# Attention scores as three row-tiled products per head, two heads at a time, in a fused attention and mixture-of-experts kernel

## The chip, the cores and the metric

The kernel runs on one core of a Trainium2 chip. The metric is the device time of one execution in microseconds, as a median over runs. TensorE (PE in the profile) multiplies; its weight loads are shown apart as PEld. VectorE is DVE, ScalarE is ACT, GpSimd is POOL, SyncE is SP.

## The reference

A normalised x attends to a context of 512 rows per batch: 16 query heads in 4 groups, head size 64. Then comes a layer of 32 experts, of which each token takes 8.

```python
def xattn(q, k, v, Wc, bc):                       # 16 batches, 512 queries, 512 keys
    qh = q.reshape(b, s, 4, 4, 64).transpose(0, 2, 3, 1, 4)
    kh = k.reshape(b, s, 4, 64).transpose(0, 2, 1, 3)
    vh = v.reshape(b, s, 4, 64).transpose(0, 2, 1, 3)
    scores = jnp.einsum('bghsd,bgtd->bghst', qh, kh) / sqrt(64)
    probs = jax.nn.softmax(scores, axis=-1)
    out = jnp.einsum('bghst,bgtd->bghsd', probs, vh)
    return out.transpose(0, 3, 1, 2, 4).reshape(b, s, 1024) @ Wc.T + bc
x = x + xattn(layernorm(x), ctx, ctx, Wc, bc)
x = x + moe(layernorm(x))                         # top 8 of 32 experts, 1024 -> 384 -> 1024
```

## The kernel before

It has four stages: a setup, attention, a schedule of expert tiles, and the experts. The change touches attention alone.

Attention works through 64 tiles of 128 queries, 4 to a batch. The first and the last batch are written out, the 14 between are turns of a loop whose body holds 4 tiles. Every engine has its own program, and each walks the 16 heads of a tile as steps h = 0 to 15. Semaphores alone tie the engines together.

Scores need more precision than one product of type fp32r gives, so queries and keys are split into a high and a low part. Of each head, qT holds the high part on array rows 0 to 63 and the low part on rows 64 to 127. The keys stand twice: kT has high over low, kT_swapped low over high. Two products over all 128 rows (lines 798 and 799) then give all four partial products of one head.

What TensorE does in step h, in this order:

- scores of head h + AHEAD, with AHEAD = 3: two products of 512 columns into bank h % 2 of two (S_BANK). It waits until the exponent of head h + 1, which read that bank last, is done.
- transpose_probs (line 813): four transposes of the probabilities of head h.
- in odd steps, values (line 836): half of the product of probabilities and values of the group before. Its output has 64 partitions, and two of these products stand side by side in the 64-column halves of the array.
- as tables of steps say, project (line 855): three products of 512 columns for each 128 rows of the output projection of the tile before, here one such chunk in most steps, two in steps 7 and 8, none in 5 and 6; then transposes of the second normalised rows (line 871, steps 4 and 5), the router (line 877, step 6), and transposes of the next tile's queries (line 776, steps 10 to 13).

What ScalarE does in step h: copy_probs (line 487, except in steps 1, 5, 9, 13, where VectorE does it on line 607), the exponent of head h + 3 (line 479), then extras: the high part of the output (496) in steps 1, 5, 9, 13, the second norm (502) in step 3, copies of its transposes (509) in 4 and 5, the next first norm (448) in 6, the high part of the next queries (455) in 7, and copies of their transposes (460) in 10 to 13.

What VectorE does in step h: the maximum of head h + 3 (line 592), then extras: 607 and the low part of the output (621, after ScalarE's 496) in steps 1, 5, 9, 13; statistics (570, 574) in 1, 2, 11 and 15; the choice of experts (642 to 652) in 7, (658) in 11, (665) in 13; places and entries of the table in 3 and 5; the residual (632) in 8 and 15. GpSimd does the low part of the next queries (393), the bias (399), small norm factors and scatters.

Of the kernel before, what the change touches and what calls it, by code (L numbers as in the profile page):

```python
# [56 lines left out]
def moe_block(nc, x, ctx_in, Wc, bc, gate_w, gate_proj, up_proj, down_proj, out):  # L57
# [36 lines left out]
    with top:  # L94
# [13 lines left out]
        with attention_mem:  # L108
# [17 lines left out]
            xq = sb(attention_mem, "xq", [P, H, 2, HEAD_DIM], F32R)  # L126
# [3 lines left out]
            kT = sb(attention_mem, "kT", [P, G, 512], F32R)  # L130
            kT_swapped = sb(attention_mem, "kT_swapped", [P, G, 512], F32R)
# [54 lines left out]
            scores_done, max_ready, exp_ready = sem("scores_done"), sem("max_ready"), sem("exp_ready")  # L186
# [167 lines left out]
            def _(pool):  # L354
# [35 lines left out]
                def queries_lo(i):  # L390

                    hold(xq_hi_ready, i + 1)
                    pool.tensor_tensor(xq[:, :, 1, :], xn[:, :].rearrange("p (h d) -> p h d", d=HEAD_DIM),
                                       xq[:, :, 0, :].bitcast(F32), ALU.subtract).then_inc(xq_ready, 1)
# [49 lines left out]
            def _(act):  # L444
# [6 lines left out]
                def queries_hi(i):  # L451

                    act.wait_ge(xn_ready, i + 1)
                    wait(act, qt_done, 4 * i)
                    act.activation(xq[:, :, 0, :], xn[:, :].rearrange("p (h d) -> p h d", d=HEAD_DIM), ACT.Copy
                                   ).then_inc(xq_hi_ready, 1)
# [110 lines left out]
            def _(dve):  # L567
# [14 lines left out]
                def keys_lo(b, g, half):  # L582

                    dve.wait_ge(khi_copied, 2 * (G * b + g) + half + 1)
                    rows = slice(half * HEAD_DIM, (half + 1) * HEAD_DIM)
                    lo, hi = (kT_swapped, kT) if half == 0 else (kT, kT_swapped)
                    dve.tensor_tensor(lo[rows, g, :], O_BANK[g % 2][rows, :], hi[rows, g, :].bitcast(F32), ALU.subtract
                                      ).then_inc(klo_copied, 1)

                def maximum(i, h):  # L590
                    dve.wait_ge(scores_done, H * i + h + 1)
# [106 lines left out]
                def tile(t):  # L698
                    i = t.i
                    for h in range(H):  # L700
# [4 lines left out]
                        for b, g in groups_at(t, h - 1, KEYS):  # L705
                            keys_lo(b, g, 1)
# [10 lines left out]
                        for b, g in groups_at(t, h, KEYS):  # L717
                            keys_lo(b, g, 0)
# [25 lines left out]
                for g in range(2):  # L744
                    for half in range(2):
                        keys_lo(0, g, half)
# [17 lines left out]
            def _(pe):  # L764
                def transpose_queries(i, n):
# [23 lines left out]
                def scores(b, s, i, h):  # L789
# [4 lines left out]
                    if h % 4 == 0 and s == 0:  # L794
                        pe.wait_ge(khi_copied, 2 * (G * b + g + 1))
                        pe.wait_ge(klo_copied, 2 * (G * b + g + 1))
# [875 lines left out]
```

## Time and profile before

| what | us |
|---|---|
| median of 3 runs | 9384.93 |
| lowest and highest | 9379.66, 9392.39 |
| the profiled execution | 9424.62 |
| its span | 9422.8 |
| PE busy, share of the span | 97% |
| DVE, ACT, POOL busy | 68%, 45%, 56% |

The profile is of one execution, 0.4% over the median. An engine counts as busy from an instruction's start to its end, and matmuls overlap each other's ends, so PE's throughput is read from the starts of its instructions and not from their durations.

### The profile page before, as it was taken

Reading aid. Unit: us, or ns where it says so; the run is one execution under the profiler, and the core shown is the slowest. Engines: PE = TensorE matmul, PEld = TensorE weight load, DVE = VectorE, ACT = ScalarE, POOL = GpSimd, SP = SyncE. Lnnn points to the kernel's source line nnn. Section 1 sums busy time; section 2 is a strip of 40 time slices with the busy share of each in tenths; the row PEclk is TensorE's granted clock in tenths of the full one; section 3 lists DMA queues with packets and bytes.
Section 4 is the critical chain, followed back from the end, with each engine's and each line's share of the span. In section 5 each row is a group of like instructions: output and inputs, shape, how many; then the busy total and the mean of one; then the engine's idle time right before and its main releaser. Section 6 shows DMA issues by size and latency. Waiting matters only on the chain.

```text
span 9422.8 us, 173720 instructions
## 1 busy us (share of the span) xinstructions
PE 9114.1 (97%) x46640; PEld 7509.9 (80%) x46641; DVE 6400.5 (68%) x9216; ACT 4227.1 (45%) x7011; POOL 5243.0 (56%) x4825
## 2 busy tenths in 40 slices
PE   8999999999969999999999999999999999999999
PEld 5777777777747888888888888888888888888888
DVE  5666666666646767777666667677777667766676
ACT  6666666666633433333333333333333333333333
POOL 2444444444445656666556566565666566656564
PEclk9999999999979999999999999999999999999999
DMA  2222212112114545555454455455555455544554
GB/s 96 59 57 59 61 55 63 58 55 64 57 60 105 117 106 115 116 124 128 109 111 110 111 132 114 108 113 114 117 116 127 105 121 114 116 107 111 127 113 82
DMA packets 787085, 926.16 MB, mean 98 GB/s; under 512 B 403473, under 2 KB 600081, under 8 KB 786578
## 3 DMA queue, kind: packets, MB, share of 16 engines
q0 software_dynamic: 209920, 604.72, 29.8%
q1 hardware_dynamic: 430866, 165.82, 7.1%
q10 hardware_dynamic: 145920, 151.01, 5.0%
q8 instruction: 184, 3.01, 0.1%
q14 instruction: 195, 1.60, 0.1%
HBM read 1076.32 MB, written 376.45 MB: 154 GB/s over the span
## 4 chain that ended last, share of the span: by engine, by line
PE 63%; DVE 3%; issue 2%; ACTq 1%; another core or an unknown queue 0%; ACT 0%; POOL 0%; DMA 0%; DVEq 0%; SPq 0%; POOLq 0%
PE bank L1581 41%; PE bank L1604 22%; DVE gu_lo L1495 1%; DVE xT L1484 1%; DVE xT_lo L1489 0%; ACTq L1383 0%; DVE h L1507 0%; DVE h_hi L1510 0%; DVE h_lo L1512 0%; ACTq L1375 0%; POOL xg L1329 0%; ACT xT_hi L1396 0%; DVE d_lo L1500 0%; DVE rows_out L1519 0%
## 5 line engine op out<-in xcount | busy, mean ns | idle before, releaser
L1329 POOL DMA_INDIRECT xg<-xn_rows,gather_row x2304 | 2970.1, 1289 | 1882.5 <-PE bank L1581 1271.4
L1581 PE MATMUL bank<-xT_hi,gu_hi 128*128 128x512 f32 (+2 forms) x6912 | 2557.1, 370 | 118.2 <-DVE xT_lo L1489 107.7
L1581 PE MATMUL bank<-xT_lo,gu_hi 128*128 128x512 f32 (+2 forms) x6912 | 2544.6, 368 | 0.0
L1581 PE MATMUL bank<-xT_hi,gu_lo 128*128 128x512 f32 (+2 forms) x6912 | 2544.5, 368 | 0.0
L1414 ACT ACTIVATE gated<-bank 128x512 f32<-128x512 f32 x432 | 258.6, 599 | 3047.0 <-PE bank L1581 2826.9
L1581 PEld LDWEIGHTS bank<-xT_hi,gu_hi 128*128 128x128 f32 x6912 | 1300.4, 188 | 302.1 <-issue 95.7
L1341 POOL DMA_INDIRECT out_rows<-rows_out,entry_now x576 | 1101.7, 1913 | 682.3 <-DVE rows_out L1519 399.0
L1581 PEld LDWEIGHTS bank<-xT_lo,gu_hi 128*128 128x128 f32 x6912 | 1300.7, 188 | 158.2
L1581 PEld LDWEIGHTS bank<-xT_hi,gu_lo 128*128 128x128 f32 x6912 | 1300.1, 188 | 158.8
L1604 PE MATMUL bank<-d_hi,h_hi 128*128 128x512 f32 x3162 | 1247.1, 394 | 53.7 <-DVE h_lo L1512 41.8
L1484 DVE STREAM_TRANSPOSE xT<-xg 128x512 f32<-128x512 f32 x1152 | 1284.1, 1156 | 13.6 <-DMA xg<-xn_rows,gather_row 13.6
L1604 PE MATMUL bank<-d_hi,h_lo 128*128 128x512 f32 x3162 | 1235.8, 391 | 0.0
L1604 PE MATMUL bank<-d_lo,h_hi 128*128 128x512 f32 x3162 | 1235.4, 391 | 0.0
L592 DVE TENSOR_REDUCE neg_max<-bank 128x1 f32<-128x512 f32 x1024 | 703.7, 687 | 568.0 <-PE bank L799 464.2
L1495 DVE TENSOR_TENSOR gu_lo<-gu_raw,gu_hi 128x2048 fp32r<-128x2048 f32 x432 | 973.5, 2284 | 151.0 <-ACT gu_hi L1403 90.6
L1507 DVE TENSOR_TENSOR h<-bank,gated 128x512 f32<-128x512 f32 x432 | 296.9, 687 | 1105.7 <-ACT gated L1414 913.2
L411 POOL DMA_INDIRECT slot_table<-entry,slot_i x512 | 507.8, 992 | 706.1 <-ACT pT L487 530.8
L479 ACT ACTIVATE probs<-bank,neg_max 128x512 f32<-128x512 f32 x1024 | 701.9, 685 | 344.8 <-DVE neg_max L592 300.5
L1403 ACT ACTIVATE gu_hi<-gu_raw 128x2048 fp32r<-128x2048 f32 x432 | 809.3, 1908 | 58.3 <-DMA gu_raw<-in_L_ffn_up_proj 58.3
L1519 DVE TENSOR_SCALAR rows_out<-bank,entry_now 128x512 f32<-128x512 f32 x576 | 430.8, 748 | 583.6 <-PE bank L1604 580.8
L1396 ACT ACTIVATE xT_hi<-xT 128x512 fp32r<-128x512 f32 x1152 | 673.5, 622 | 300.9 <-issue 276.3
L1489 DVE TENSOR_TENSOR xT_lo<-xT,xT_hi 128x512 fp32r<-128x512 f32 x1152 | 750.9, 684 | 77.2 <-ACT xT_hi L1396 77.2
(160 smaller groups left out, 12733.6 us busy)
## 6 DMA issues: line engine op xcount, KB each, us to landing
d_raw<-in_L_ffn_down_proj ACTq DMA_DIRECT2D x144, 1536.0 KB
gu_raw<-in_L_ffn_gate_proj ACTq DMA_DIRECT2D x145, 1024.0 KB
gu_raw<-in_L_ffn_up_proj ACTq DMA_DIRECT2D x145, 1024.0 KB
gu_raw<-in_L_ffn_gate_proj ACTq DMA_DIRECT2D x145, 512.0 KB
gu_raw<-in_L_ffn_up_proj ACTq DMA_DIRECT2D x145, 512.0 KB
xg<-xn_rows,gather_row POOLq DMA_INDIRECT x2304
x_t<-in_x SPq DMA_DIRECT2D x64, 512.0 KB, 4.8
inv_wide<-inverse_sums SPq DMA_DIRECT2D x512, 64.0 KB
```

The lines of the kernel that those rows point to most:

```text
L411: pool.indirect_dma_start(out=table, out_offset=bass.IndirectOffsetOnAxis(ap=slot_i[:, k:k + 1], axis=0), in_=entry[:, k, :], in_offset=No ...
L479: act.activation(probs[h % 4][:, :], S_BANK[h % 2][:, :], ACT.Exp, bias=neg_max[:, h:h + 1], accum_out=row_sum[:, h:h + 1]).then_inc(exp_r ...
L592: dve.tensor_reduce(neg_max[:, h:h + 1], S_BANK[h % 2][:, :], AX.X, ALU.max, negate=True).then_inc(max_ready, 1)
L1329: pool.indirect_dma_start(out=xg[:, m, :], out_offset=None, in_=quarter_rows, in_offset=bass.IndirectOffsetOnAxis(ap=gather_row[:, m:m + 1 ...
L1341: pool.indirect_dma_start(out=out, out_offset=bass.IndirectOffsetOnAxis(ap=entry_now[:, q, 0:1], axis=0), in_=rows_out[:, q, :], in_offset ...
L1396: act.activation(xT_hi[:, c, :], xT[:, c, :], ACT.Copy).then_inc(xt_hi, 1)
L1403: act.activation(gu_hi[:, :, :, cols], gu_raw[:, :, :, cols].rearrange("p n c m -> p c n m"), ACT.Copy).then_inc(guhi_ready, 1)
L1484: dve.transpose(xT[:, :, 2 * pair * QUAD:2 * (pair + 1) * QUAD].rearrange("p c (m r) -> p m c r", r=QUAD), xg[:, 2 * pair:2 * pair + 2, :] ...
L1489: dve.tensor_tensor(xT_lo[:, c, :], xT[:, c, :], xT_hi[:, c, :].bitcast(F32), ALU.subtract).then_inc(xt_lo, 1)
L1495: dve.tensor_tensor(gu_lo[:, :, :, cols], gu_raw[:, :, :, cols].rearrange("p n c m -> p c n m"), gu_hi[:, :, :, cols].bitcast(F32), ALU.su ...
L1581: last = nc.tensor.matmul(bank[:, 0:cols], w[:, c, n, j * P:(j + 1) * P], v[:, c, 0:cols], start=(c == 0 and w is gu_hi and v is xT_hi), s ...
L1604: last = nc.tensor.matmul(D_BANK[q][n][:, 0:cols], v[:, k, q * P:(q + 1) * P], w[:, k, n * 512:n * 512 + cols], start=(k == ks[0] == 0 and ...
```

## The change

Queries: xq keeps the whole high row and then the whole low row, no longer side by side for each head. One transpose of 128 columns then holds two heads, the even one on rows 0 to 63 and the odd one on rows 64 to 127; qT[:, h] of an even h is the high part of both and qT[:, h + 1] their low part. Keys: the high part stands on both halves of kT_hi, the low part on both halves of kT_lo; ScalarE writes the one in one instruction (two before), VectorE the other in one (two before).

Scores come two heads at a time, in odd steps: high by high, high by low and low by high of each head, each over 64 array rows, the even head into bank 0 and the odd head into bank 1. The low by low product is gone. The call waits for the exponents of both heads that used the banks before.

The step order of TensorE changes: scores and the query transposes of an odd step come first in it; two chunks of the projection stand in every even step, at its end, behind the transposes of the second norm and the router.

```diff
-            PROJECT = {0: (1, 0, 1, 2), 1: (1, 0, 2, 3), 2: (1, 0, 3, 4), 3: (1, 0, 4, 5), 4: (1, 0, 5, 6), 7: (1, 0, 6, 8),
-                       8: (1, 1, 0, 2), 9: (1, 1, 2, 3), 10: (1, 1, 3, 4), 11: (1, 1, 4, 5), 12: (1, 1, 5, 6), 13: (1, 1, 6, 7),
-                       14: (1, 1, 7, 8), 15: (0, 0, 0, 1)}
+            PROJECT = {h: (1, h // GROUP_HEADS // 2, h % 8, h % 8 + 2) for h in range(0, H, 2)}
...
-                    act.activation(kT[0:HEAD_DIM, g, :], O_BANK[g % 2][0:HEAD_DIM, :], ACT.Copy).then_inc(khi_copied, 1)
-                    act.activation(kT_swapped[HEAD_DIM:P, g, :], O_BANK[g % 2][HEAD_DIM:P, :], ACT.Copy).then_inc(khi_copied, 1)
+                    act.activation(kT_hi[:, g, :], O_BANK[g % 2][:, :], ACT.Copy).then_inc(khi_copied, 1)
...
+                    dve.tensor_tensor(kT_lo[:, g, :], O_BANK[g % 2][:, :], kT_hi[:, g, :].bitcast(F32), ALU.subtract
...
-                                                   xq[:, 4 * n + k, :, :].rearrange("p two d -> p (two d)"), ident_r[:, :])
+                                                   xq[:, k % 2, (2 * n + k // 2) * P:(2 * n + k // 2 + 1) * P], ident_r[:, :])
...
-                    wait(pe, exp_ready, H * i + h - 1)
-                    nc.tensor.matmul(S_BANK[h % 2][:, :], qT[s % 2][:, h, :], kT[:, g, :], start=True, stop=False)
-                    nc.tensor.matmul(S_BANK[h % 2][:, :], qT[s % 2][:, h, :], kT_swapped[:, g, :], start=False, stop=True
-                                     ).then_inc(scores_done, 1)
+                    wait(pe, exp_ready, H * i + h)
+                    for part, keys in ((0, kT_hi), (0, kT_lo), (1, kT_hi)):
+                        for r in range(2):
+                            rows = slice(HEAD_DIM * r, HEAD_DIM * (r + 1))
+                            last = nc.tensor.matmul(S_BANK[r][:, :], qT[s % 2][rows, h + part, :], keys[rows, g, :],
+                                                    start=(part == 0 and keys is kT_hi), stop=(part == 1))
+                            if part == 1:
+                                last.then_inc(scores_done[r], 1)
...
                     for h in range(H):
-                        if h + AHEAD < H:
-                            scores(t.b, t.s, i, h + AHEAD)
-                        elif t.next:
-                            scores(t.next_b, t.next_s, i + 1, h + AHEAD - H)
+                        if h % 2:
+                            scores_ahead(t, h)
+                            queries_at(t, h)
                         transpose_probs(i, h)
...
-                        if h in PROJECT and (t.back1 or not PROJECT[h][0]):
-                            back, n, c0, c1 = PROJECT[h]
-                            project(i - back, n, list(range(c0, c1)))
                         if h in TRANSPOSE2 and t.back2:
                             transpose_xn2(i - 2, TRANSPOSE2.index(h))
                         if h == ROUTER and t.back2:
                             router(i - 2)
-                        if h in NEXT_QUERIES and t.next:
-                            transpose_queries(i + 1, NEXT_QUERIES.index(h))
+                        if h % 2 == 0:
+                            project_at(t, h)
+                            queries_at(t, h)
```

On TensorE, steps 3 and 4 of a tile, without their first and last rows, stood like this before (798 and 799 are scores, 813 transposes of probabilities, 836 values, 855 the projection, 871 transposes of the second norm):

```order
L813 MATMUL bank<-ident,probs 128x128 x4
L836 MATMUL bank<-pT,v 64x256 x4
L855 MATMUL bank<-WcT_hi,oT_hi 128x512
L855 MATMUL bank<-WcT_lo,oT_hi 128x512
L855 MATMUL bank<-WcT_hi,oT_lo 128x512
L41 REGISTER_ALU
L798 MATMUL bank<-kT,qT 128x512
L799 MATMUL bank<-kT_swapped,qT 128x512
L41 REGISTER_ALU
L813 MATMUL bank<-ident,probs 128x128 x4
L855 MATMUL bank<-WcT_hi,oT_hi 128x512
```

The same place now, steps 3 and 4 (791 is scores, 807 the transposes of probabilities, 830 values, 865 those of the second norm, 849 the projection):

```order
L791 MATMUL bank<-kT_hi,qT 128x512 x2
L791 MATMUL bank<-kT_lo,qT 128x512 x2
L791 MATMUL bank<-kT_hi,qT 128x512 x2
L807 MATMUL bank<-ident,probs 128x128 x4
L830 MATMUL bank<-pT,v 64x256 x4
L807 MATMUL bank<-ident,probs 128x128 x4
L865 MATMUL bank<-ident,xn 128x128 x4
L849 MATMUL bank<-WcT_hi,oT_hi 128x512
L849 MATMUL bank<-WcT_lo,oT_hi 128x512
```

Scores, transposes, values and transposes now follow each other, and the projection stands in one piece behind them, just ahead of the next scores.

ScalarE's order does not change in these steps; of the changed kernel, steps 7 and 8 (474 exponent, 452 high part of the next queries, 482 copy of transposed probabilities):

```order
L474 ACTIVATE probs,row_sum<-bank,neg_max 128x512
L41 REGISTER_ALU
L452 ACTIVATE xq<-xn 128x1024
L482 ACTIVATE pT<-bank 128x4x128
L470 REGISTER_ALU
L474 ACTIVATE probs,row_sum<-bank,neg_max 128x512
```

The exponent at the end of this piece is the one for which TensorE's scores of step 9 now wait; before, it was the one at its head.

## Rows read from the trace of the kernel before

**Rows 1.** Stretches: start:end, length, busy PE, PEld, DVE, ACT, POOL, clock, DMA share, GB/s.

```profile
144.00:2723.00 2579.00, 2502.41 (x15730) 1851.87 (x15729) 1695.88 (x3837) 1709.29 (x3816) 1117.95 (x1846) 0.99 0.20 58
1350.00:1397.70 47.70, 42.66 (x261) 31.05 (x261) 30.70 (x68) 30.74 (x69) 18.13 (x30) 0.96 0.15 49
1397.70:1437.10 39.40, 39.40 (x252) 29.24 (x251) 27.06 (x61) 27.19 (x61) 18.20 (x30) 1.00 0.17 52
```

**Rows 2.** Timeline (start us, length us, instruction, [idle before]), PE: the router, once a tile.

```profile
1437.14 1.91 PE L877 MATMUL bank<-gate_sb,xn2T 128*128 128x32 f32 x16
1476.65 1.91 PE L877 MATMUL bank<-gate_sb,xn2T 128*128 128x32 f32 x16
```

**Rows 3.** Timeline, PE: steps 8 and 9 of an ordinary tile.

```profile
1442.97 0.60 PE L813 MATMUL bank<-ident,probs 128*128 128x128 f32 x4
1443.32 0.48 PE L855 MATMUL bank<-WcT_hi,oT_hi 128*128 128x512 f32 x1
...
1445.03 0.39 PE L799 MATMUL bank<-kT_swapped,qT 128*128 128x512 f32 x1
1445.26 0.60 PE L813 MATMUL bank<-ident,probs 128*128 128x128 f32 x4
1445.79 1.08 PE L836 MATMUL bank<-pT,v 128*64 128x256 f32 x8
1446.81 0.50 PE L855 MATMUL bank<-WcT_hi,oT_hi 128*128 128x512 f32 x1
1447.14 0.40 PE L855 MATMUL bank<-WcT_lo,oT_hi 128*128 128x512 f32 x1
```

**Rows 4.** Groups by line in attention: weight loads of 64 and of 128 columns.

```profile
L836 PEld LDWEIGHTS bank<-pT,v 128*64 128x64 f32 x3960 | 241.0, 136 | 156.2 <-issue 84.9
L799 PEld LDWEIGHTS bank<-kT_swapped,qT 128*128 128x128 f32 x982 | 187.0, 190 | 24.6
```

**Rows 5.** Timeline, ACT, of the same tile.

```profile
1441.30 1.06 ACT L455 ACTIVATE xq<-xn 128x1024 fp32r<-128x1024 f32 x1
1443.60 0.60 ACT L487 ACTIVATE pT<-bank 128x512 f32<-128x512 f32 x1 [1.24 <-PE bank L813]
1444.10 0.68 ACT L479 ACTIVATE probs<-bank,neg_max 128x512 f32<-128x512 f32 x1
1444.66 0.20 ACT L479 ACTIVATION_READ_ACCUMULATOR probs<-bank,neg_max 128x1 f32 x1
...
1446.19 0.69 ACT L479 ACTIVATE probs<-bank,neg_max 128x512 f32<-128x512 f32 x1 [1.04 <-DVE neg_max L592]
...
1446.87 0.41 ACT L496 ACTIVATE oT_hi<-o_norm 128x256 fp32r<-128x256 f32 x1
...
1471.36 1.23 ACT L502 ACTIVATE xn<-x,ln 128x1024 f32<-128x1024 f32 x1
```

**Rows 6.** Timeline, DVE, of the same tile.

```profile
1445.46 0.69 DVE L592 TENSOR_REDUCE neg_max<-bank 128x1 f32<-128x512 f32 x1 [0.68 <-issue]
1446.07 0.68 DVE L607 COPY pT<-bank 128x512 f32<-128x512 f32 x1
1447.30 1.50 DVE L621 TENSOR_TENSOR oT_lo<-o_norm,oT_hi 128x256 fp32r<-128x256 f32 x1 [0.56 <-ACT oT_hi L496]
...
1457.36 0.42 DVE L621 TENSOR_TENSOR oT_lo<-o_norm,oT_hi 128x256 fp32r<-128x256 f32 x1 [0.69 <-issue]
1457.70 0.60 DVE L665 TENSOR_REDUCE chosen<-hot 128x32 bf16<-128x256 f32 x1
...
1460.78 0.68 DVE L632 TENSOR_TENSOR x<-bank,x_t 128x512 f32<-128x512 f32 x1
1462.34 0.21 DVE L574 BATCH_NORM_AGGREGATE mv<-bn 128x2 f32<-128x12 f32 x1 [0.16 <-DVE bn L570]
```

**Rows 7.** Timeline, POOL, of the same tile.

```profile
1446.11 2.40 POOL L399 TENSOR_TENSOR x_t<-x_t,bias_row 128x1024 f32<-128x1024 f32 x1
```

**Rows 8.** Timeline, DVE, where the loop turns.

```profile
1548.85 0.69 DVE L592 TENSOR_REDUCE neg_max<-bank 128x1 f32<-128x512 f32 x1 [4.72 <-issue]
```

More of the change, by code:

```diff
@@ L125, in moe_block @@
             xn = sb(attention_mem, "xn", [P, D], F32)
-            xq = sb(attention_mem, "xq", [P, H, 2, HEAD_DIM], F32R)
+            xq = sb(attention_mem, "xq", [P, 2, D], F32R)
             qT = [sb(attention_mem, f"qT{n}", [P, H, P], F32R) for n in range(2)]
@@ L129, in moe_block @@
             v = sb(attention_mem, "v", [P, TC, G, HEAD_DIM], F32)
-            kT = sb(attention_mem, "kT", [P, G, 512], F32R)
-            kT_swapped = sb(attention_mem, "kT_swapped", [P, G, 512], F32R)
+            kT_hi = sb(attention_mem, "kT_hi", [P, G, 512], F32R)
+            kT_lo = sb(attention_mem, "kT_lo", [P, G, 512], F32R)
             probs = [sb(attention_mem, f"probs{n}", [P, 512], F32) for n in range(4)]
@@ L184, in moe_block @@
             khi_copied, klo_copied = sem("khi_copied"), sem("klo_copied")
-            scores_done, max_ready, exp_ready = sem("scores_done"), sem("max_ready"), sem("exp_ready")
+            scores_done, max_ready, exp_ready = [sem(f"scores_done{n}") for n in range(2)], sem("max_ready"), sem("exp_ready")
             inverse_turned = sem("inverse_turned")
@@ L454, in queries_hi @@
                     wait(act, qt_done, 4 * i)
-                    act.activation(xq[:, :, 0, :], xn[:, :].rearrange("p (h d) -> p h d", d=HEAD_DIM), ACT.Copy
-                                   ).then_inc(xq_hi_ready, 1)
+                    act.activation(xq[:, 0, :], xn[:, :], ACT.Copy).then_inc(xq_hi_ready, 1)
                 def copy_queries(i, s, n):
@@ L580, in statistics1, with keys_lo @@
                     statistics(n, ln1_chain, 2 * i, bn1, mv1, x_t[s], stats1)
[L582 to L587, printed above, removed]
+                def keys_lo(b, g):
+                    dve.wait_ge(khi_copied, G * b + g + 1)
+                    dve.tensor_tensor(kT_lo[:, g, :], O_BANK[g % 2][:, :], kT_hi[:, g, :].bitcast(F32), ALU.subtract
                                       ).then_inc(klo_copied, 1)
                 def maximum(i, h):
-                    dve.wait_ge(scores_done, H * i + h + 1)
+                    dve.wait_ge(scores_done[h % 2], H // 2 * i + h // 2 + 1)
                     dve.tensor_reduce(neg_max[:, h:h + 1], S_BANK[h % 2][:, :], AX.X, ALU.max, negate=True
@@ L704, in tile @@
                             maximum(i + 1, h + AHEAD - H)
-                        for b, g in groups_at(t, h - 1, KEYS):
-                            keys_lo(b, g, 1)
                         if t.back1 and h == RESIDUAL[0]:
@@ L717, in tile @@
                         for b, g in groups_at(t, h, KEYS):
-                            keys_lo(b, g, 0)
+                            keys_lo(b, g)
                         if t.back3:
@@ L744, in _ @@
                 for g in range(2):
-                    for half in range(2):
-                        keys_lo(0, g, half)
+                    keys_lo(0, g)
                 for h in range(AHEAD):
@@ L830, in values @@
                         if keys is not None:
-                            pe.wait_ge(klo_copied, 2 * keys)
+                            pe.wait_ge(klo_copied, keys)
                         if s == 0:
@@ L887, in ranks, with scores_ahead, project_at, queries_at @@
                                      ).then_inc(rank_done, 1)
+                def scores_ahead(t, h):
+                    if h + AHEAD < H:
+                        scores(t.b, t.s, t.i, h + AHEAD)
+                    elif t.next:
+                        scores(t.next_b, t.next_s, t.i + 1, h + AHEAD - H)
+                def project_at(t, h):
+                    if h in PROJECT and (t.back1 or not PROJECT[h][0]):
+                        back, n, c0, c1 = PROJECT[h]
+                        project(t.i - back, n, list(range(c0, c1)))
+                def queries_at(t, h):
+                    if h in NEXT_QUERIES and t.next:
+                        transpose_queries(t.i + 1, NEXT_QUERIES.index(h))
                 def tile(t):
@@ L920, in _ @@
                     transpose_queries(0, n)
-                for h in range(AHEAD):
+                for h in (0, 2):
                     scores(0, 0, 0, h)
@@ L925, in _ @@
                 ranks(LAST - 2)
-                project(LAST, 0, list(range(1, 4)))
+                project(LAST, 0, list(range(0, 4)))
                 project(LAST, 1, list(range(0, 4)))
```

7 lines of the change are left out of this document (3 added, 4 removed).

## Prediction, made before the run

> **What bounds the kernel now.** The busy time by stretch comes first. Attention takes 2,579 us of the span. In an ordinary tile of it PE is busy 39.4 of 39.4 us, at full clock; DVE and ACT are busy 27 [rows 1]. From router to router such a tile takes 39.5 us [rows 2]. So attention is bound by PE's order, without a wait, except where its loop turns: there a tile takes 47.7 us with PE idle for 5 [rows 1], and DVE has a hole of 4.7 us that nothing but issue explains [rows 8]. Of 64 tiles I count 48 as ordinary and 15 as turns. The change can gain only what it takes out of PE's order, and loses wherever it makes that order wait.
>
> Next, starts in the timeline of PE [rows 3]. A score or projection product costs 0.23 to 0.24 us. Four transposes of probabilities start 0.11 apart (0.60 in all, one lasting 0.27). Then the values: 8 matmuls of 256 columns in 1.08 us, the next kind 1.02 after the first. At the transposes' rate of 0.11 for 128 columns, 8 such matmuls in turn would take 1.75; they run in pairs, about 0.22 a pair. Entering this two-tile form costs: the last transpose starts at 1445.59, the first of the values at 1445.79, so 0.20 instead of 0.11; the last pair starts 0.70 after the first where three pairs are 0.65, so 0.05 goes to weights not loaded ahead. Leaving it costs too: the projection starts 0.32 after the last pair instead of 0.22, and its second product 0.33 later instead of 0.24. Between fp32 transposes and fp32r products of the full array I find no such loss: after four transposes the projection starts at once (0.35 after the first of them).
>
> **The change on PE.** Two heads cost 4 products of 0.234 us before, 0.94. Now they cost 3 pairs of about 0.22 if the two row halves run side by side, 0.65, plus entering and leaving a tiled form once more, in all 8 times a tile. By the rows of the values: draining before 0.09, draining after 0.10, weights not loaded ahead. The weights are 128 columns, not 64 (0.190 against 0.136 us, so 0.05 more than the 0.05 seen) [rows 4], and about 0.06 more for the weights of the transposes behind, an estimate from the 0.11 that the projection's cost there. That is 0.35, so a block of 1.00 us against 0.94: +0.06, bounded below by 3 pairs without any switch (-0.29) and above by six products in turn, 1.40 + 0.35 (+0.81).
> TensorEngine Tiling (Array Packing) of the Trainium skill, under Key Properties, says that changing the tiling mode drains the engine. This speaks against the change: 8 more entries a tile; the rows on the values agree for the column form, and no row shows the row form. TensorE: Matmul & The Clock Gate of the Trainium skill, Part 3, gives 3.07 times for four row tiles; by that share a pair would cost 0.30 instead of 0.22 and the kernel, as an estimate, some 130 us more.
> What it saves besides: behind the values now come transposes, whose weights are cheaper to load late (0.05 x 8), and some query transposes fall between blocks (0.3 a tile). Sum for PE without waits: 39.1 us a tile against 39.5. That is -0.4, or -26 us in 64 tiles. Where batches meet, ACT and DVE each save 4 instructions of 0.6 to 0.7 us; they lie beside PE and I count nothing for them.
>
> **The change in waiting.** Before, the scores of step h waited for an exponent of ScalarE's step h - 2, two whole steps of cover. Now the block of an odd step h waits for the exponent of ScalarE's step h - 1, and that stands behind copy_probs of h - 1, which needs the transposes that PE has just made. Queued behind the waiting block are transposes, values and all else. The only cover is the projection. I walk one pair of steps, block start at 0:
> PE: block to 0.84, transposes (last starts at 1.22), values from 1.42, second transposes from 2.44 (last at 2.82), six products from 2.85, next block at 4.41.
> ACT: a copy starts 0.31 after the last transpose (1443.30 to 1443.60), the exponent 0.50 after that, and its sum is done 0.76 after its start, the block 0.05 later [rows 3, 5]: 2.82 + 0.31 + 0.50 + 0.76 + 0.05 = 4.44.
> DVE: the first maximum starts 0.43 after the last score product, at 0.96, and holds DVE for 0.61; the exponent follows a maximum's start by 0.72 (1445.46 to 1446.19) [rows 3, 5, 6]. So a second maximum that starts at x lets the next block start at x + 1.53; x may be 2.9.
> The plain period is thus just balanced, and every extra of an odd step lies on the path. Per period, named by its odd step:
> - 1: copy 1.70, ACT's output split from 2.35 (0.68 behind the exponent at 1.67), DVE's part from 2.79, done 3.14 (0.34 later), statistics 0.66: x = 3.80, block at 5.33. PE alone 4.51.
> - 3: the second norm starts at 2.70, lasts 1.23 [rows 5], and its transposes now stand ahead of the projection: they start near 4.0, not 2.9. Block at 6.05, PE alone 4.85.
> - 5: the router waits for the copies of those transposes, 0.45. 7.05, PE alone 6.6.
> - 7: the queries' high part, 1.06 [rows 5], pushes copy_probs from 3.13 to 3.69: 5.0, PE alone 4.41.
> - 9: DVE's split lasted 1.50 instead of 0.42, as long as GpSimd's bias addition ran [rows 6, 7]. GpSimd's chain starts from the queries' high part; the addition falls 4.8 us behind that (1441.30 to 1446.11), so at 7.5 to 9.9 of period 7, and DVE's split would be due at 7.8: it ends near 10.0, x = 5.0, block at 6.55. PE alone 4.69.
> - 11: 4.95, PE's own.
> - 13: split and choice (0.60): x = 3.79, 5.3. PE alone 4.69.
> - 15: residual, statistics, aggregate (1460.78 to 1462.55, 1.77) [rows 6]: x = 3.44, 4.97. PE alone 4.41.
> Sum 45.2 us a tile against 39.5: +5.7, of which 6.1 are waits. Times 48: +274 us. Where the loop turns, DVE's hole lies in period 15 and wholly on the path: 45.2 + 4.7 = 49.9 at least against 48. If the old excess of 9 stays whole it is 54. I take +3.5, times 15: +53. The sum is +327 us.
> The walk is made against the profiled execution of 9,424.6 us, which would become 9,752; the median of the runs lies 40 us lower, so I forecast **9,710 us**.
>
> The waits are the weak term. If the collision of step 9 does not happen, 1.85 a tile go (-118 us). If each chain is 0.3 us shorter than walked, 2 a tile (-130). If the collision catches other splits too, or the loop turn costs 10 more, +150. The experts' stage (6,600 us) is untouched.
>
> **The rivals.**
> A, the halves do not run side by side. The values show pairs for column tiles alone, and in fp32, while these are fp32r on row tiles; against it speaks only that likeness. Each block costs 0.75 more, and every chain hangs on its last product: 8 x 0.75 x 64 = +384, so 10,095 us.
> B, faster. Going to row tiles costs nothing, so 0.36 less a block and 2.9 less a tile, and ACT and DVE keep up since each has 12 us of 39 to spare. The whole of it is 39.1 - 2.9 = 36.2 us a tile, 3.3 x 64 = 211 us gained: 9,175 us. It decides at the waits: with a free switch, faster only while they stay under 3.3 us a tile; I walk to 6.1. With 2 us of them it is 9,300.
> C, the waits do not come, because query transposes, router and projection cover them, and the switch costs what it does for the values: -26 us at best, 9,360, to +30 when a pair costs 0.234.
>
> **How the numbers follow.** My forecast has 0.80, and its own bounds are 9,480 to 9,960 (half of the waits at the low end; the collision more often, weights of the two halves loaded in turn, 0.11 x 8 x 64 = 55 us, and the full turn at the high end). A has 0.07, B 0.07, C 0.06. The range 9,480 to 9,960 leaves out these three, 0.20. A measurement of this kernel tells about 0.2% (19 us) from no change. Faster: B and a third of C, 0.09. Same: 0.04 out of C. Slower: the rest, 0.87.
>
> **What would show it.** Right: ordinary tiles of 43 to 47 us, PE idle ahead of the score blocks with ACT's exponent as what ended it, and ahead of the second norm's transposes with ACT's norm; three starts of pairs 0.22 apart, and 0.3 from the last pair to the transposes; the experts' stage the same. Wrong: row pairs that start 0.23 apart each (A); tiles under 39 us (B); PE without idle time at 39 us (C). If a tile is near 45 us but the wait is elsewhere, the walk and not its sum was wrong.

## The result, and the profile after

| | before | after |
|---|---|---|
| median, us | 9387.16 (4 runs) | 9771.17 (4 runs) |
| lowest and highest, us | 9379.66, 9392.39 | 9768.36, 9771.55 |
| span of the profiled execution, us | 9422.8 | 9769.4 |

The changed kernel is slower: ratio 1.0409, 95% interval 1.0391 to 1.0427, some 384 us. I had forecast 9,710 us; it is 61 us more.

Busy time by stretch, of the changed kernel: attention, the experts' stage, an ordinary tile, a part of that tile, and a tile where the loop turns. The columns are start:end, length, and the busy time of each engine with its number of instructions.

```profile
core 0: us, PE busy (x) PEld busy (x) DVE busy (x) ACT busy (x) POOL busy (x), PEclk, DMA share, GB/s
144.00:3100.00 2956.00, 2617.09 (x16789) 1738.59 (x16786) 1703.58 (x3785) 1677.50 (x3771) 1120.92 (x1858) 0.98 0.18 51
3196.00:9769.00 6573.00, 6504.31 (x30320) 5579.81 (x30320) 4604.73 (x5174) 2434.28 (x3022) 4048.36 (x2864) 1.00 0.52 114
1208.70:1255.80 47.10, 42.16 (x268) 27.76 (x266) 27.59 (x62) 26.84 (x61) 18.26 (x30) 0.96 0.15 47
1223.80:1227.20 3.40, 3.40 (x18) 2.16 (x19) 1.91 (x4) 0.82 (x2) 0.71 (x1) 0.54 0.02 1
1156.20:1208.70 52.50, 45.49 (x282) 30.55 (x282) 28.88 (x64) 29.06 (x67) 18.10 (x30) 0.93 0.14 42
```

From the first score product to the last, attention took 2,637 us before and takes 3,019 now: +382. That is as much as the medians differ. The two profiled executions differ by 347 us only: in the one of the kernel before, the experts' stage, which the change does not touch, took 6,607 us, 34 more than the 6,573 here. Most of the 37 us by which that execution lay above its median are thus outside attention. In an ordinary tile, which PE filled without a gap before [rows 1], it is now busy 42.2 of 47.1 us. From router to router an ordinary tile takes 47.2 us (29 of them) or 45.7 (16), against 39.5 [rows 2]; a tile where the loop turns takes 50.5 to 52.5 against 48.0 (medians 50.9 and 48.0).

Who waited for whom on PE in attention (total in us, times, longest), after, and behind the dots the two largest of before:

```profile
PE bank L791 <- ACT probs L474: 230.8, 284, 2.1
PE bank L865 <- ACT xn L497: 70.3, 62, 2.1
PE bank L807 <- issue: 22.3, 13, 2.0
PE bank L871 <- ACT xn2T L504: 12.4, 48, 0.7
...
PE bank L798 <- ACT probs L479: 39.0, 25, 2.9
PE bank L871 <- ACT xn L502: 32.1, 15, 2.6
```

The three waits that the prediction named are there: score blocks (line 791) for ScalarE's exponents, the second norm's transposes (865) for its norm, the router (871) for its copies. They come to 313 us, against 73 before. The view counts from the end of the last product, which lies up to 0.17 us behind the start of what could have followed it, so it shows less than the periods below.

### The profile page after: what moved, and what is told of

Read it like the earlier page. It is cut to its first block, busy times and chain, and to the rows that moved or that the text cites. A ratio compares the mean times of both kernels' runs of the same rounds, so it can differ in the third digit from the quotient of the medians.

```text
span 9769.4 us, 175724 instructions
## 1 busy us (share of the span) xinstructions
PE 9218.2 (94%) x47664; PEld 7383.6 (76%) x47665; DVE 6401.2 (66%) x9152; ACT 4185.8 (43%) x6947; POOL 5238.8 (54%) x4825
## 4 chain that ended last, share of the span: by engine, by line
PE 63%; DVE 1%; issue 1%; ACTq 1%; ACT 0%; POOL 0%; DMA 0%; DVEq 0%; SPq 0%; POOLq 0%
PE bank L1590 42%; PE bank L1613 21%; DVE xT_lo L1498 0%; ACTq L1392 0%; ACTq L1384 0%; ACT xT_hi L1405 0%; POOL xg L1338 0%; DVE rows_out L1528 0%; DVE gu_lo L1504 0%; ACTq L1382 0%; DVE xT L1493 0%; DVE h L1516 0%; DVE h_lo L1521 0%; DVE h_hi L1519 0%; DMA entry_in<-slot_table 0%
```

## The walk against the trace

The timeline of PE in one ordinary tile: around the blocks of steps 9 and 11, and the second norm's transposes in step 4 (start, length, instruction, idle before).

```profile
1216.26 0.40 PE L849 MATMUL bank<-WcT_hi,oT_lo 128*128 128x512 f32 x1
1217.11 0.50 PE L791 MATMUL bank<-kT_hi,qT 64*128 64x512 f32 x2 [0.45 <-ACT probs L474]
1217.44 0.40 PE L791 MATMUL bank<-kT_lo,qT 64*128 64x512 f32 x2
1217.67 0.40 PE L791 MATMUL bank<-kT_hi,qT 64*128 64x512 f32 x2
1218.00 0.66 PE L807 MATMUL bank<-ident,probs 128*128 128x128 f32 x4
...
1223.80 0.57 PE L791 MATMUL bank<-kT_hi,qT 64*128 64x512 f32 x2 [1.85 <-ACT probs L474]
1224.17 0.63 PE L791 MATMUL bank<-kT_lo,qT 64*128 64x512 f32 x2
1224.60 0.63 PE L791 MATMUL bank<-kT_hi,qT 64*128 64x512 f32 x2
...
1225.70 1.07 PE L807 MATMUL bank<-ident,probs 128*128 128x128 f32 x4
...
1249.99 0.66 PE L865 MATMUL bank<-ident,xn 128*128 128x128 f32 x4 [0.88 <-ACT xn L497]
```

The two row halves do run side by side: two products of 512 columns stand in one row of 0.40 us, and the next pair starts 0.23 later. A block takes 0.89 us to the transposes behind it; I had 0.84, since I took 0.22 for a pair.

Period by period, the time from one block to the next, named by the odd step in which it begins. The measured column is the median over 40 ordinary tiles of the changed kernel.

| period | PE alone, as worked out | forecast | measured | what ended it |
|---|---|---|---|---|
| 1 | 4.51 | 5.33 | 5.32 | exponent |
| 3 | 4.85 | 6.05 | 6.02 | second norm, ahead of its transposes |
| 5 | 6.6 | 7.05 | 7.23 | copies, ahead of the router |
| 7 | 4.41 | 5.0 | 5.01 | exponent |
| 9 | 4.69 | 6.55 | 6.69 | exponent |
| 11 | 4.95 | 4.95 | 6.60 | PE itself, at half clock |
| 13 | 4.69 | 5.3 | 5.47 | exponent |
| 15 | 4.41 | 4.97 | 4.79 | exponent |

Seven of eight are within 0.2 us. Period 9 has the cause that I gave it. The timelines of VectorE, GpSimd and ScalarE there:

```profile
1219.95 2.39 DVE L614 TENSOR_TENSOR oT_lo<-o_norm,oT_hi 128x256 fp32r<-128x256 f32 x1 [0.55 <-ACT oT_hi L491]
1222.26 0.68 DVE L585 TENSOR_REDUCE neg_max<-bank 128x1 f32<-128x512 f32 x1
...
1219.64 2.41 POOL L396 TENSOR_TENSOR x_t<-x_t,bias_row 128x1024 f32<-128x1024 f32 x1
...
1222.97 0.69 ACT L474 ACTIVATE probs<-bank,neg_max 128x512 f32<-128x512 f32 x1 [2.08 <-DVE neg_max L585]
```

VectorE's split (the low part of the output, line 614) takes 2.39 us and ends 0.29 us after GpSimd's bias addition (1222.34 and 1222.05); it was 0.42 elsewhere [rows 6, 7]. In the whole trace 63 of 256 splits are this long. They are those that meet such an addition, and each ends 0.29 us after it. The maximum follows it, the exponent the maximum, the block the exponent.

Period 11 is what I did not see. After the wait of 1.85 us the pairs start 0.43 apart, twice the usual 0.23, and four transposes take 1.07 us in place of 0.66. The granted clock of that stretch is 0.54: the lower of its two levels, 1.2 instead of 2.4 GHz. In attention the clock records show 38 such stretches, 130 us together; before there were 9, 34 us. Half of the 96 us more is lost where PE is the bound: up to 48 us. The tiles tell the same: period 11 is 6.67 us in the tiles with such a stretch (28 of 47 ordinary ones) and 5.12 in the others, which is what makes the two lengths of tile. 28 times 1.55 is 43 us.
TensorE: Matmul & The Clock Gate of the Trainium skill describes such a fall of the clock when TensorE goes idle in "HAM oscillation — how this bites in real kernels". Its example waits longer, for DMA; here 1.85 us, after a period with 0.45 us idle, was enough in three tiles of five. The prediction has no term for it.

## The experiments

Each was timed in rounds with the kernel before. The table has four groups, each timed together on one chip: the changed kernel, the next four rows, the four behind them, and the last three. The kernel before took 9,387, 9,399, 9,438 and 9,397 us beside them. So medians of different groups must not be subtracted from each other; ratios can be compared, and so can attention in the profiled executions (from the first score product to the last, 2,637 us before). The experts' stage, the same in all, took 6,569 to 6,580 us in the second group's traces and 6,606 to 6,629 in the third's. The expectations start from the 9,771 us of the changed kernel. Periods are medians over some 40 ordinary tiles.

| kernel | median, us | ratio to before, interval | attention, us | ordinary tile, us |
|---|---|---|---|---|
| changed kernel | 9771 | 1.0409, 1.0391 to 1.0427 | 3019 | 47.2 or 45.7 |
| second maximum early | 9534 | 1.0145, 1.0128 to 1.0162 | 2775 | 42.1 |
| bias late | 9626 | 1.0245, 1.0228 to 1.0262 | 2869 | 43.7 |
| order alone | 9750 | 1.0376, 1.0358 to 1.0393 | 2985 | 44.9 or 46.4 |
| heads in turn | 9784 | 1.0413, 1.0396 to 1.0431 | 3017 | 47.2 or 45.7 |
| projection first | 9708 | 1.0287, 1.0264 to 1.0309 | 2921 | 44.2 to 45.7 |
| block behind values | 10087 | 1.0687, 1.0665 to 1.0708 | 3287 | 48.8 to 51.8 |
| the same, early maximum | 9899 | 1.0482, 1.0456 to 1.0507 | 3100 | 45.6 to 48.7 |
| the same, all edits | 9601 | 1.0170, 1.0149 to 1.0190 | 2807 | 42.7 |
| four places | 9404 | 1.0010, 1.0001 to 1.0019 | 2648 | 40.2 |
| values first | 9471 | 1.0079, 1.0065 to 1.0093 | 2707 | 41.1 |
| four places, full array | 9431 | 1.0030, 1.0018 to 1.0043 | 2665 | 40.5 |

### Is it the order or the row form?

The first question is whether the new products cost the time at all. This kernel has the old ones, in the new order.

```diff
-                    wait(pe, exp_ready, H * i + h - 1)
-                    nc.tensor.matmul(S_BANK[h % 2][:, :], qT[s % 2][:, h, :], kT[:, g, :], start=True, stop=False)
...
+                    wait(pe, exp_ready, H * i + h)
+                    for r in range(2):
+                        nc.tensor.matmul(S_BANK[r][:, :], qT[s % 2][:, h + r, :], kT[:, g, :], start=True, stop=False)
```

> The kernel before with its layout and its two full-array products per head, but in the changed kernel's order on TensorE: two heads at a time in odd steps, waiting for both exponents, and the projection in even steps. Theory (the order makes the waits and the row form costs about what it saves): a block is 0.94 instead of 1.00, all chains stay, so 9,700 to 9,790 us. Rival (the row-tiled products or their switches cost the time): back near 9,390 us.

It took 9,750 us, a ratio of 1.0376 against 1.0409; in attention it is 35 us below the changed kernel. The order alone makes nine tenths of the loss, and the rival that blamed the row form falls. Period 9 is 6.69 us here too. The waits on PE are the same ones:

```profile
PE bank L797 <- ACT probs L477: 194.7, 229, 3.1
PE bank L870 <- ACT xn L500: 70.3, 63, 2.0
```

Period 11 has a median of 5.09 us here, behind the same long wait in 9: the half clock comes in only 11 of 46 ordinary tiles, against 28 of 47. A wait of this length is followed by it at times and not at others, and what decides that stays open.

Not all chains are as long as in the changed kernel, though. With the old products the even head is ready after two of them, and VectorE's first maximum starts 0.77 us after the block; with the row form both heads end together, and it starts at 1.00. The periods that hang on VectorE are shorter by that: 13 is 5.19 and not 5.47, period 1 is 5.10 and not 5.32.

### VectorE between the two maxima

```diff
-                        if h + AHEAD < H:
-                            maximum(i, h + AHEAD)
-                        elif t.next:
-                            maximum(i + 1, h + AHEAD - H)
+                        for ahead in (AHEAD, AHEAD + 1) if h % 2 else ():
+                            if h + ahead < H:
+                                maximum(i, h + ahead)
+                            elif t.next:
+                                maximum(i + 1, h + ahead - H)
```

> The changed kernel, with one edit on VectorE: the maxima of both heads of a pair stand one behind the other at the start of an odd step, ahead of that step's other work. Theory (VectorE's extras between the two maxima are what the next score block waits for): periods 1, 9, 13 and 15 fall from 5.32, 6.69, 5.47 and 4.80 us to 4.5 to 4.8, and with the 1.9 us wait of period 9 gone the half clock of period 11 (6.57) goes too. 5 us a tile, so some 9,430 to 9,500 us. Rival (ScalarE's own order, copy then exponent, sets the block's start, and the maxima are ready anyway): under 1 us a tile, 9,700 to 9,770. Second rival (the row-tiled products are what costs): no change, 9,771.

Measured 9,534 us where I expected 9,430 to 9,500, so it missed: attention is 244 us shorter, not 270 to 340. Periods 1, 9, 11, 13 and 15 fell to 4.56, 4.78, 5.11, 4.84 and 4.58 us, close to the 4.5 to 4.8 expected for four of them, and the stretches at half clock from 38 to 10. Together that is 5.1 us a tile against the long tiles and 3.6 against the short; the loop's turns gained less, 50.9 to 48.3, and the short tiles are what I had left out. VectorE's split still takes 2.4 us in step 9, but nothing waits for it any more (VectorE's timeline):

```profile
1042.47 2.41 DVE L614 TENSOR_TENSOR oT_lo<-o_norm,oT_hi 128x256 fp32r<-128x256 f32 x1
```

What PE still waits for in a tile of this kernel:

```profile
1025.43 0.66 PE L866 MATMUL bank<-ident,xn 128*128 128x128 f32 x4 [0.88 <-ACT xn L497]
...
1031.25 1.97 PE L872 MATMUL bank<-gate_sb,xn2T 128*128 128x32 f32 x16 [0.25 <-ACT xn2T L504]
...
1039.64 0.50 PE L792 MATMUL bank<-kT_hi,qT 64*128 64x512 f32 x2 [0.46 <-ACT probs L474]
```

These are periods 3, 5 and 7, the ones that I had put on ScalarE.

### GpSimd and VectorE at once

```diff
-            NEXT_STATS, NEXT_FACTORS, NEXT_NORM, NEXT_SPLIT, NEXT_QUERIES, NEXT_BIAS = (1, 2), 2, 6, 7, (10, 11, 12, 13), 8
+            NEXT_STATS, NEXT_FACTORS, NEXT_NORM, NEXT_SPLIT, NEXT_QUERIES, NEXT_BIAS = (1, 2), 2, 6, 7, (10, 11, 12, 13), 15
```

> The changed kernel, with one number changed: GpSimd adds the bias in step 15 and not in step 8. Theory (VectorE's split of step 9 is held while GpSimd's bias addition runs, 2.39 us instead of 0.42): period 9 falls from 6.69 to about 4.8 us and the half clock behind it goes, so period 11 from 6.57 to 4.98; 3.4 us a tile, 9,550 to 9,620 us in all. Where the addition now meets another split, up to half of that comes back. Rival (the split is long for another reason): 9,771, with L614 still at 2.4 in step 9.

Measured 9,626 us, 6 above what was expected, and 150 less in attention. All four splits of an ordinary tile now take 0.42 or 0.43 us. Here are the split of step 9, and the bias addition, which now comes 13 us behind it:

```profile
1028.23 0.43 DVE L614 TENSOR_TENSOR oT_lo<-o_norm,oT_hi 128x256 fp32r<-128x256 f32 x1 [0.56 <-ACT oT_hi L491]
...
1041.27 2.39 POOL L396 TENSOR_TENSOR x_t<-x_t,bias_row 128x1024 f32<-128x1024 f32 x1
```

Period 9 fell from 6.69 to 4.78, period 11 from 6.60 to 5.11 with the clock at 1.00; no other moved. One number in a table of steps is thus worth some 150 us here, and it worked in two ways: the hold itself and the clock behind it.

### The second norm and the router

```diff
+                        if h % 2 == 0:
+                            project_at(t, h)
                         if h in TRANSPOSE2 and t.back2:
                             transpose_xn2(i - 2, TRANSPOSE2.index(h))
                         if h == ROUTER and t.back2:
                             router(i - 2)
                         if h % 2 == 0:
-                            project_at(t, h)
                             queries_at(t, h)
```

> The changed kernel with the projection of an even step ahead of the transposes of the second norm and of the router, as the kernel before had it. Theory (in period 3 the transposes wait for ScalarE's norm because nothing stands ahead of them, in period 5 the router waits for the copies): period 3 falls from 6.02 to about 5.1 us, period 5 from 7.23 to about 6.8; 1.3 us a tile, so 9,680 to 9,710 us. Rival (the norm or the exponent behind it would be late all the same): both periods as they were, 9,771.

Period 3 fell from 6.02 to 5.19, period 5 from 7.23 to 6.63. The 9,708 us lie in the expected range, but the kernel before was slower on this chip too: by the ratios, 1.0287 against 1.0409, and by attention, 98 us less, the gain is 100 us and more and not the 61 to 91 expected. Part of it is clock: the half clock follows period 9 in 13 of 46 ordinary tiles, where the changed kernel had it in 28 of 47. The projection covers the wait for the norm, 70 us before and 7 now, and the router's is gone.

### Two heads in turn

> The changed kernel with the six products of a block in another order: three of the even head, then three of the odd head, so that no two of different row halves stand next to each other but once. Theory (two row halves run at once only when their products are neighbours): a block goes from 1.00 to between 1.5 and 1.7 us, 0.5 to 0.7 x 8 x 64, so 10,030 to 10,140 us. Rival (the pair starts in the trace are only how records are written, and the products run in turn in both): 9,771 us.

```diff
-                    for part, keys in ((0, kT_hi), (0, kT_lo), (1, kT_hi)):
-                        for r in range(2):
+                    for r in range(2):
+                        for part, keys in ((0, kT_hi), (0, kT_lo), (1, kT_hi)):
```

This expectation missed, in an instructive way. The time is the same, 9,784 us (ratios 1.0413 and 1.0409), and so is the block:

```profile
707.23 0.50 PE L791 MATMUL bank<-kT_hi,qT 64*128 64x512 f32 x2 [0.57 <-ACT probs L474]
707.57 0.39 PE L791 MATMUL bank<-kT_lo,qT 64*128 64x512 f32 x2
707.80 0.40 PE L791 MATMUL bank<-kT_hi,qT 64*128 64x512 f32 x2
708.13 0.66 PE L807 MATMUL bank<-ident,probs 128*128 128x128 f32 x4
```

Three products of one row half stand ahead of the other half's in the program, yet the trace shows them start in pairs, 0.01 us apart or less (one row of 0.39 us holds two of them), and the transposes come 0.90 us after the block's start. The two row halves ran through their products next to each other whatever the order. I expected this run to show what the block costs without the pairs, and it does not; that a pair is only an artefact of the records is excluded by the time to the transposes, since six products in turn at 0.23 would need 1.4 us.

### More cover by a later block

```diff
-                        if h % 2:
-                            scores_ahead(t, h)
-                            queries_at(t, h)
                         transpose_probs(i, h)
                         if h % GROUP_HEADS in VALUE_CHUNKS:
...
+                        if h % 2:
+                            scores_ahead(t, h)
+                            queries_at(t, h)
```

> The changed kernel with the score block behind the transposes and values of its odd step instead of ahead of them. It gives the exponent that the block waits for 1.5 us more, and goes from the column form straight to the row form, one switch less. Theory (VectorE's chain through both maxima is as long as before, only ScalarE's part is covered): period 7 falls from 5.01 to about 4.6 us, the periods with long VectorE work by 0.1 to 0.2; 1 to 2 us a tile, 9,640 to 9,710 us. Rival (missing cover on PE is the whole matter): the waits go, 9,370 to 9,450.

> Both at once: the block behind the values, and both maxima at the start of VectorE's odd step. Theory (the two chains, VectorE's and ScalarE's, are all that holds a block; what stays is the second norm and PE's own work): 39.5 to 41 us a tile, 9,330 to 9,460 us. Rival (some third chain, such as transposed copies or the loop's turn, takes their place): no better than the early maxima alone, 9,534.

> The block behind the values, both maxima early, the projection ahead of the second norm's transposes and the router, and the bias addition in step 15. Theory (PE is bound by its own work again, which is 39.1 us a tile less 0.2 for each switch saved): 37.5 to 39.5 us a tile, 9,260 to 9,390 us, so it may beat the kernel before. Rival (waits of 0.3 us and more stay in most periods): above 9,390.

All three missed, and the first two are slower than the changed kernel: 1.0687 and 1.0482 against its 1.0409. The waits of the first on PE in attention:

```profile
PE bank L791 <- ACT probs L474: 203.1, 232, 1.8
PE bank L865 <- ACT xn L497: 163.2, 63, 3.7
PE bank L871 <- ACT xn2T L504: 79.1, 64, 1.4
```

The score blocks' wait fell by 28 us only: periods 1, 13 and 15, which hang on VectorE's chain from the block through both maxima, are as long as they were. But the wait for the norm rose from 70 to 163 us, for the router's copies from 12 to 79, and periods 3 and 5 from 6.02 and 7.23 to 8.60 and 9.75.

Two things are in these numbers. In the 12 tiles in which no stretch at half clock falls into period 3, it is 7.12 us, and period 5 without one is 8.18: so 1.1 and 0.95 us are the lateness itself. The reading for it is that the other engines begin an odd step with the block's maximum, so that all they do in that step comes later as PE sees it; no run takes this apart. The rest, some 1.6 us in each of the two periods, is clock. The stretches at half clock rose from 38 to 131, and half of what they add is up to 200 us, of the 268 that attention lost against the changed kernel.

With early maxima periods 3 and 5 stayed at 8.67 and 9.76; with all edits they were 5.83 and 8.11, and there PE waits up to 1.3 us for VectorE's low part of the output, and 0.9 for its copy of the logits, ahead of the projection. Cover on PE had been bought with lateness elsewhere, and with clock.

### Taking the waits out one by one

> The changed kernel with its waits taken out one by one and the score block left ahead of the values: both maxima early, the projection ahead of the second norm's transposes and the router, the bias addition in step 15, and ScalarE's and GpSimd's split of the next queries in step 8 instead of 7. Theory (each wait has its own cause, so the gains add): periods 4.45, 4.8, 5.1, 4.8, 4.6, 4.6, 5.1 and 6.6 us, 40.1 a tile, 9,400 to 9,450 us. Rival (they cover each other, and taking out one uncovers the next): above 9,500.

```diff
-            NEXT_STATS, NEXT_FACTORS, NEXT_NORM, NEXT_SPLIT, NEXT_QUERIES, NEXT_BIAS = (1, 2), 2, 6, 7, (10, 11, 12, 13), 8
+            NEXT_STATS, NEXT_FACTORS, NEXT_NORM, NEXT_SPLIT, NEXT_QUERIES, NEXT_BIAS = (1, 2), 2, 6, 8, (10, 11, 12, 13), 15
```

Beside this it has the early maxima and the projection first, as above. It took 9,404 us, within what was expected, and an ordinary tile 40.2 us where I expected 40.1. The periods are 4.51 (7), 4.78, 5.11, 4.84, 4.58, 4.55, 5.19 and 6.63 us. Behind its first tiles, not one stretch at half clock is left in attention. Period 7, which the early maxima, the late bias and the projection first had each left at 5.01, is 4.51 here, so the later split of the queries is what shortened it. An ordinary tile:

```profile
1000.00:1040.20 40.20, 39.97 (x270) 27.29 (x268) 25.64 (x61) 26.25 (x62) 18.35 (x30) 1.00 0.18 54
```

The next edit puts the values first as well:

```diff
-                        transpose_probs(i, h)
...
+                        if h % 2 and h != 5:
+                            values_at(t, h)
+                        if h % 2:
+                            scores_ahead(t, h)
+                            queries_at(t, h)
+                        transpose_probs(i, h)
```

> As the version with four places changed, and the values ahead of the score block in odd steps, except in step 5. Unlike the block behind transposes and values, this leaves VectorE's and ScalarE's next work as close to the block as it was. It saves the switch from the column form to the full array and back (0.16 us) in seven of eight periods and gives the block 1 us of cover. Theory: 39.0 us a tile and cheaper loop turns, 9,320 to 9,400 us, about as fast as the kernel before or faster. Rival (whatever made the late block slow, also does here): above 9,450.

This version missed: 9,471 us, 41.1 a tile. Four periods are shorter by 0.13 to 0.25 (4.62 in 9, 4.67 in 13, 4.33 in 15, 4.42 in 1), so the saved switch is there. But period 3, which has no values in it any more, is still 5.19, and period 5, which has two halves of them, 7.64; period 7 is 5.05 instead of 4.51. What PE waits for in attention shows where:

```profile
PE bank L866 <- ACT xn L497: 50.3, 63, 1.6
PE bank L792 <- ACT probs L474: 31.5, 62, 0.6
PE bank L850 <- DVE logits L635: 27.9, 62, 0.5
```

It now comes early to the second norm's transposes (50 us of waits against 11 in the version with four places) and to the projection of step 8, whose bank VectorE must have emptied of the logits. It looks like the late block's fault in a milder form.

> The kernel before with its two full-array products per head, in the order of the version with four places changed. With the waits mostly gone, the difference to that version is what the row form is worth on a busy PE. Theory (a block of 1.00 against 0.94 us): 0.05 to 0.1 a block, 25 to 50 us less than that version, 9,360 to 9,420. Rival (the row form saves a quarter of the products' time, 0.24 a block): 100 us and more above that version.

The old products in the order of the four places took 9,431 us, against 9,404 with the row form, and no run of the one reaches into the runs of the other. My sign was wrong. How much the row form is worth is less sure: attention differs by 17 us in the two traces, and the experts' stage, which no edit touches, by 21. So it is some 17 to 27 us, 0.2 or 0.3%.

What PE itself pays is best read where the block waits for nothing, in steps 5 and 7. The block of step 7 of the changed kernel, and one of the version with the order alone:

```profile
1211.77 0.40 PE L849 MATMUL bank<-WcT_hi,oT_lo 128*128 128x512 f32 x1
1212.10 0.50 PE L791 MATMUL bank<-kT_hi,qT 64*128 64x512 f32 x2
...
1212.99 0.66 PE L807 MATMUL bank<-ident,probs 128*128 128x128 f32 x4
...
1049.60 0.39 PE L854 MATMUL bank<-WcT_hi,oT_lo 128*128 128x512 f32 x1
1049.83 0.39 PE L797 MATMUL bank<-kT,qT 128*128 128x512 f32 x1
1050.06 0.39 PE L798 MATMUL bank<-kT_swapped,qT 128*128 128x512 f32 x1
...
1050.76 0.60 PE L812 MATMUL bank<-ident,probs 128*128 128x128 f32 x4
```

The row form starts 0.33 us after the projection's last product and not 0.23 (the drain), takes 0.89 and not 0.93 to the transposes, and these take 0.66 and not 0.60. That is 0.12 us dearer a block. But where the block has waited, the old form pays as well. PE's timeline of the block of step 5 in the full-array version goes from 1025.12 to 1026.16:

```profile
1025.12 0.50 PE L798 MATMUL bank<-kT,qT 128*128 128x512 f32 x1 [0.20 <-ACT probs L477]
1025.46 0.39 PE L799 MATMUL bank<-kT_swapped,qT 128*128 128x512 f32 x1
...
1026.16 0.60 PE L813 MATMUL bank<-ident,probs 128*128 128x128 f32 x4
```

That is 1.04 us against the row form's 0.90: its second product comes 0.34 behind the first, not 0.23, and the row form's drain lies in the wait. Nearly every block of this version takes 1.00 to 1.04 us. So in periods with a small wait left the row form wins 0.04 to 0.09 (7, 1, 15, 3, 13), and in the others it is 0.01 to 0.05 behind (5, 9, 11).

## Why the prediction was right, point by point

- **The bound before and the untouched stage.** PE was without a gap in attention, and the medians differ by what attention lost. The 40 us that I took off for the slow profiled execution were rightly taken off, since 34 of them lie in the experts' stage.
- **The block on PE.** Forecast 1.00 against 0.94 with side-by-side pairs. They run side by side; a block takes 0.89 to the transposes and not 0.84. With the drain of 0.10 and the 0.06 behind it, it is 1.05 against 0.93 where nothing waits, so the cost was twice the 0.06 worked out. That the order alone is 35 us shorter in attention than the changed kernel, close to the 31 that 0.06 a block would give, is partly luck: later first maxima and more half clock are in it too.
- **Rival A** falls: a block is 0.89 us to the transposes, and six products in turn would need 1.4. Its sign was badly worded: the pairs do start 0.23 us apart, and what decides is that each start is of two products.
- **Rival B** falls as well: the switches are there (0.33 us ahead of the pairs and 0.33 from the last pair to the transposes), and the periods stand some 6 us a tile above what was worked out for PE alone, clock aside, far above the 3.3 where it turned.
- **The drain.** The rule on tiling modes of TensorEngine Tiling (Array Packing) in the Trainium skill holds in the row form too: 0.10 us ahead of a block that waits for nothing. From the values I had 0.09.
- **The waits.** The walk gave 6.1 us a tile. Seven periods come within 0.2 us. The experiments took its causes away: VectorE's extras in one, the collision with GpSimd in one, the norm and the router together in one, and the queries' high part in the version with four places.
- **The loop's turn.** Forecast 3.5 us more; measured 2.9.
- **What was short.** The step on period 11 said "PE's own, 4.95". It was 6.60, since PE ran at half clock behind the wait of period 9; at full clock it was 5.12. The clock's term was missing, not mis-sized: 43 to 48 of the 61 us. The rest is spread over PE's own work in period 11 (0.17) and periods 9, 5 and 13 (0.14 to 0.18 each), less 0.18 in period 15 and the loop's turns.
- **PE without waits.** The sum said 39.1 us a tile, less than before. No run reached it: with four places changed PE is busy 39.97 of 40.2 us, above the 39.4 of before. The forecast did not hang on this, since the waits cover it in most periods.
- **The rival with late waits hidden (C)** fell for the kernel as it is. The version with four places shows what it would have needed, and even there it is no faster than before: 1.0010. Its upper end was also added up wrongly: a pair of 0.234 costs 0.05 us more a block, 27 us in all, so it ends near no change and not at +30. In the same way half of the walked waits is 195 us and gives 9,515 as the low end, not 9,480. Neither bears on the account above.

## What to carry to other kernels

Letting an engine wait for work of the step before, and not of the step before that, costs nothing as long as the chain of that work is shorter than what covers it. Write down that chain for every step, with each engine's extras in it, and compare it with the work that covers it. When a wait of this kind is to go, pull the work that is waited for forward on the engine that is late (here one VectorE instruction, 244 us of attention); pushing the waiting work back made other work late here, and brought more half clock. A wait of 1.85 us on TensorE cost 1.55 us more in clock behind it, in three tiles of five, so the longest waits are worth more than their length. And compare runs of different groups by their ratios: the kernel before took 9,387 us in one and 9,438 in another.

## What the runs showed of the hardware beyond what was expected

- Two row halves of the array work through their products side by side even when three of the one stand ahead of the three of the other: starts within 0.01 us of each other, a block of 0.90 us in either order, ratios 1.0413 and 1.0409.
- Two fp32r products of 512 columns over 64 rows each, side by side, take 0.23 us, as one over 128 rows does. Going from the full array to the row form costs 0.10 us ahead of the first pair.
- The second product of a block came 0.34 us behind the first where the block had waited, and 0.23 where it had not, in the full-array form.
- A VectorE subtraction of 128 x 256, 0.42 us alone, took 2.39 while GpSimd's addition of 128 x 1024 ran and ended 0.29 us after it, in 63 cases of the changed kernel's trace; it took 0.43 when the addition was moved away. Maxima and copies from the banks kept their 0.69 and 0.68.
- Behind a wait of 1.85 us TensorE's granted clock was 0.54 for a stretch, in 28 of 47 ordinary tiles, and behind a wait of 1.77 us in 11 of 46 with the order alone; with the wait gone (bias late), in none.
